# The end of the gap between two scans: 1 + e in another buffer, product buffers in the other order, the second row norm on VectorE, GpSimd's list in another order

## What is computed

```python
# mixer (per batch, channels in 8 blocks of 128, 16 states n)
delta = softplus(dt_w @ dt + dt_b)                    # (512, 1024)
h = h * exp(delta * A[n]) + (delta * u) * B[n]        # scan over 512 steps
y = sum_n h * C[n] + u * D ; y = y * silu(z) ; x = x + y @ out_w
# quantised MLP on layernorm(x), weights of this batch
x = x + smooth_quant_mlp(layernorm(x), fside, ctx)
# experts on layernorm(x): this is "the second row norm"
x = x + top2_of_16_experts(layernorm(x)) + sigmoid(gate) * shared_expert(layernorm(x))
```

## Time and profile before

| | us |
|---|---|
| median of 3 runs | 1702.78 |
| lowest, highest | 1702.05, 1710.21 |
| profiled execution | 1698.6 |
| its span, first to last instruction | 1696.8 |
| TensorE busy in it | 1445.6 |
| VectorE busy | 1349.2 |
| GpSimd busy | 1065.7 |
| ScalarE busy | 798.0 |

### The profile page before, as it was taken

One profiled execution on the slowest core, in us unless ns is written; L12 is line 12 of the kernel. 1 busy time (PEld: TensorE's weight loads), 2 busy tenths in 40 slices (PEclk: granted clock), 3 DMA queues, 4 the chain that ended last, 5 costly groups with the idle time before them and its releaser, 6 DMA issues.

```text
span 1696.8 us, 19403 instructions
## 1 busy us (share of the span) xinstructions
PE 1445.6 (85%) x5408; PEld 830.0 (49%) x5416; DVE 1349.2 (80%) x2215; ACT 798.0 (47%) x1368; POOL 1065.7 (63%) x684
## 2 busy tenths in 40 slices
PE   7867678999699899999699899999699999836994
PEld 3323223444465565444465565444465665325783
DVE  3488999676899999796899999796899999784212
ACT  3575454245734565245734565245734565222141
POOL 0299999101999899500999899500999999422101
PEclk9988899999699999999699999999699999967997
DMA  3550000412535674513535674512534774600984
GB/s 111 207 204 25 0 0 1 161 38 76 220 121 182 198 242 150 204 44 101 217 124 174 205 238 154 204 44 101 217 125 147 236 233 130 248 25 8 353 333 143
DMA packets 94074, 252.14 MB, mean 149 GB/s; under 512 B 11024, under 2 KB 11152, under 8 KB 88848
## 3 DMA queue, kind: packets, MB, share of 16 engines
q1 hardware_dynamic: 86688, 229.93, 39.9%
q0 software_dynamic: 5120, 16.78, 3.0%
q10 hardware_dynamic: 2160, 4.19, 0.6%
HBM read 207.87 MB, written 42.99 MB: 148 GB/s over the span
## 4 chain that ended last, share of the span: by engine, by line
PE 52%; DVE 18%; issue 13%; POOL 7%; ACT 7%; DMA 2%; DVEq 0%; POOLq 0%; SPq 0%; ACTq 0%
PE bank L1902 10%; PE bank L1780 6%; DVE bank L1253 6%; PE bank L2028 5%; PE bank L1795 4%; PE bank L1834 4%; PE bank L1839 4%; POOL work L659 4%; PE bank L1931 3%; PE bank L1828 3%; PE bank L1923 2%; PE bank L1803 2%; DVE work L1265 2%; PE bank L1802 2%; DVE pairs L1265 2%
## 5 line engine op out<-in xcount | busy, mean ns | idle before, releaser
L659 POOL TENSOR_TENSOR work<-du,BB 128x1024 f32<-128x1024 f32 x255 | 603.0, 2378 | 5.2 <-DVE work L1529 4.4
L926 ACT ACTIVATE bank<-delta,A_sb 128x512 f32<-128x512 f32 x512 | 349.9, 690 | 477.3 <-DVE pairs L1265 260.8
L1253 DVE TENSOR_TENSOR_SCAN bank<-bank,work 128x512 f32<-128x512 f32 x432 | 522.5, 1219 | 12.9 <-ACT bank L926 9.2
L1902 PEld LDWEIGHTS bank<-x3T,ew_up 128*128 128x128 f32 x1488 | 221.1, 196 | 74.5 <-issue 63.2
L1902 PE MATMUL bank<-x3T,ew_up 128*128 128x128 f32 (+1 forms) x1488 | 243.3, 310 | 5.2 <-issue 5.2
L1265 DVE TENSOR_TENSOR pairs<-bank,CB 128x512 f32<-128x512 f32 x240 | 160.9, 671 | 1.6 <-PE bank L1839 0.6
L604 POOL TENSOR_TENSOR col<-col,halfpow 128x4 f32<-128x4 f32 (+1 forms) x8 | 7.8, 973 | 209.8 <-DVE col L1405 209.8
L1265 DVE TENSOR_TENSOR work<-bank,CB 128x512 f32<-128x512 f32 x192 | 128.3, 668 | 0.0
L1795 PE MATMUL bank<-xT,wst 128*128 128x512 f32 x256 | 117.7, 604 | 8.4 <-ACT delta L873 6.6
L1834 PE MATMUL bank<-pairs,ident 128*128 128x512 f32 x160 | 90.6, 650 | 34.4 <-DVE zg L1273 18.8
L2028 PE MATMUL bank<-wst,zg 128*128 128x512 f32 x256 | 117.0, 593 | 0.9 <-DVE zg L1273 0.9
(11 more groups left out here) (243 smaller groups left out, 2518.2 us busy)
## 6 DMA issues: line engine op xcount, KB each, us to landing
ew_up<-in_exp_w SPq DMA_DIRECT2D x93, 512.0 KB, 3.8
ew_dn<-in_exp_w SPq DMA_DIRECT2D x93, 256.0 KB, 4.3
hm<-xs_dram SPq DMA_DIRECT2D x69, 256.0 KB, 4.6
ys_dram<-x3T SPq DMA_DIRECT2D x69, 256.0 KB, 4.5
wst<-in_w_in SPq DMA_DIRECT2D x64, 256.0 KB, 2.7
BB<-bc_dram SPq DMA_DIRECT2D x16, 1024.0 KB, 7.2
CB<-bc_dram SPq DMA_DIRECT2D x16, 1024.0 KB, 9.1
wst<-in_out_w SPq DMA_DIRECT2D x32, 256.0 KB, 2.9
```

Of the source, the lines that this page charges most:

```text
L659: nc.gpsimd.tensor_tensor(dBu[:, k % CHUNK_SLOTS, :, :], du[:, j % 2:j % 2 + 1, :].broadcast_to([P, 2, T]), BB[:, n0:n0 + 2, :], ALU.mult) ...
L926: nc.scalar.activation(R[q % RING][:, :], delta[:, j, :], ACT.Exp, scale=A_sb[:, j, n:n + 1]).then_inc(S["da_ready"], 1)
L1253: V.tensor_tensor_scan(prod[c % (2 * PAIR_SLOTS)] if on_pool(q) else R[q % RING][:, :], R[q % RING][:, :], dBu[:, c // 2 % CHUNK_SLOTS, c ...
L1902: ins = mm(gu_bank(v)[:, part * n:(part + 1) * n], w[:, part * D + k * P:part * D + (k + 1) * P], rhs, start=(k == 0), stop=(k == KD - 1))
```

## The change

1. **Buffer of 1 + e.** `sp_w` of blocks 4 to 7 is `xT`, the transposed input, in place of `late_pairs`. `one_more` of these blocks waits for all z projections, the last readers of `xT`, no longer for `softplus_less` of blocks 0 to 3.
2. **Product buffers.** `prod[0:4]` is `late_pairs`, `prod[4:8]` is `pairs`. Products 0 to 3 wait for `softplus_less` of blocks 0 to 3 and products 4 to 7 for the errors of blocks 4 to 7.
3. **VectorE** does `softplus_less` of blocks 1 to 3 (new `less`) and the second row norm (new `row_norm`: one small step for `row_shift`, four tiles of `xn`) ahead of `one_more` of blocks 4 to 7. The errors of blocks 4 to 7 move behind products 2 and 3.
4. **GpSimd** makes only the power of the second norm, and before du and chunk 0 (`row_power`). `softplus_sum` of blocks 4 to 7 follows chunk 1, and chunk 2 waits for it and for all inverses; `softplus_less` of blocks 4 to 7 is spread to steps 4, 7, 9 and 11 of the scan's pair loop.
5. **ScalarE** loses the row norm, and its four `x3` copies stand ahead of `lns` of blocks 4 to 7.

`last`, which has no scan beside it, keeps `norm` and ScalarE's `row_norm`.

```diff
+LESS_AT = {4: 4, 5: 7, 6: 9, 7: 11}
+ERROR_AT = {4: 3, 5: 3, 6: 4, 7: 4}
-        prod = [pairs[:, i, :] for i in range(4)] + [late_pairs[:, i, :] for i in range(4)]
+        prod = [late_pairs[:, i, :] for i in range(4)] + [pairs[:, i, :] for i in range(4)]
         def sp_w(a, m):
+            return late_pairs[:, m, :] if m < 4 else xT[:, m - 4, :]
# GpSimd
+            def row_power(l):
+                pool.wait_ge(S["var_ready"], l + 1)
+                nc.gpsimd.tensor_tensor(rstd[:], mv[:, :, 1], halfpow[:, 1, :], ALU.pow).then_inc(S["rstd_ready"], 2)
             def chunk(b, k):
                 if k == 2 and b > 0:
                     pool.wait_ge(S["sum_ready"], NBLK * (b + 1))
+                    pool.wait_ge(S["sp_inv_ready"], NBLK * (b + 1))
# ScalarE, between
                 for c in range(RING):
                     decay(a, c)
+                for i in range(KD):
+                    x3(a, i)
                 lns(a, range(4, 8))
-                row_norm(m, 2 * m + 1)
                 inverses(a, range(4, 8))
# VectorE
             def one_more(a, m):
                 if m >= 4:
-                    ve.wait_ge(S["delta_ready"], NBLK * a + m - 3)
+                    ve.wait_ge(S["z_ps"], NBLK * (a + 1))
+            def less(a, m):
+                ve.wait_ge(S["sum_ready"], NBLK * a + m + 1)
+                ve.wait_ge(S["sp_err_ready"], NBLK * a + m + 1)
+                ve.wait_ge(S["delta_ready"], NBLK * a + m)
+                V.tensor_tensor(delta[:, m, :], delta[:, m, :], sp_w(a, m), ALU.subtract).then_inc(S["delta_ready"], 1)
+            def row_norm(m):
+                l = 2 * m + 1
+                ve.wait_ge(S["var_ready"], l + 1)
+                ve.wait_ge(S["rstd_ready"], 2 * (l + 1))
+                V.scalar_tensor_tensor(out=row_shift[:], in0=mv[:, :, 0], scalar=-1.0, in1=rstd[:],
+                                       op0=ALU.mult, op1=ALU.mult).then_inc(S["row_shifted"], 1)
+                ve.wait_ge(S["row_shifted"], l + 1)
+                for t in range(TT):
+                    V.tensor_scalar(xn[:, t, :], x2[:, t, :], rstd[:, t:t + 1], row_shift[:, t:t + 1], ALU.mult, ALU.add
+                                    ).then_inc(S["xn_ready"], 1)
# VectorE, scan_stage: after the product of step p
-                    if scan and p == 1 and b > 0:
-                        for i in range(4, 8):
-                            softplus(b, i)
+                    for i in range(4, 8):
+                        if scan and b > 0 and p == ERROR_AT[i]:
+                            softplus(b, i)
# VectorE, between
                 row_stats(m, 2 * m + 1)
+                for i in range(1, 4):
+                    less(a, i)
+                row_norm(m)
                 for i in range(4, 8):
                     one_more(a, i)
```

## The result

| | before | changed |
|---|---|---|
| median of 6 runs each, same chip | 1705.13 us | 1726.32 us |
| lowest, highest | 1700.33, 1710.21 | 1721.44, 1729.84 |
| ratio, 95% interval | | 1.0118 [1.0098, 1.0139] |
| profiled execution, its span | 1698.6, 1696.8 | 1728.51, 1726.8 |
| granted clock | 0.931 | 0.923 |

The time went up by 21.2 us where +9.0 was forecast; 1726.3 lies outside 1695 to 1717. The sign was right, the size less than half. What follows is counted inside the three gaps, from the end of VectorE's variance step (432.70 before, 439.06 after), and leaves that out.

A forecast was written before the change was run, and what follows sets the result against it. Two chains with next to no slack bound it: VectorE through scan 5 to `posi`, GpSimd to the gates' weights. Each 3.0 us later a gap, 9.0 in three, on 1702.8 gave 1711.8 us; range 1695 to 1717.

The forecast's parts named there:

- Row norm, the port: VectorE's moved steps and GpSimd's big ones wait for each other's whole instruction; the last tile ends at 442.3.
- free port: Rival, chance 0.15: the port hardly matters for VectorE's moved steps; -3.1 us a gap, 1693.5 us.
- row norm that slips through: Rival, chance 0.24: small step and tiles hold the port ahead of chunk 1; 1700 to 1706.5 us.
- fourth rival: Chance 0.05: GpSimd's power also blocks VectorE's first `less`; 1.3 us a gap more, 1715.7 us.
- ScalarE, part 5: ScalarE waits 3.9 us for TensorE's transposes, then makes the copies first; inverses come 3.0 us later.
- Scan and errors: On VectorE each moved error meets a long GpSimd step; scan 5 starts at 464.4 instead of 461.43, +3.0 us.
- Both chains are displaced by 3.0 us a gap: The sum: VectorE at scan 5 and GpSimd at the gates' weights each 3.0 us late, 9.0 in three gaps.
- TensorE's clock: Rival, chance 0.12: matmuls ahead of the first down projection run at 1.2 GHz; 0 to 2.8 us a gap on top.
- Not on the path: Logits and the first expert's matmuls start some 6 us earlier, but next meet VectorE's routing at fixed scan steps.
- GpSimd: Chunk 2 starts 4.5 us earlier, four `softplus_less` add 5.1, waits add more; gates' weights +3.0 us.
- Only their own time: Spreading GpSimd's four `softplus_less` over later steps costs just their duration, 4 x 1.27 = 5.1 us.
- the forecast's case: VectorE and GpSimd take turns at the port, chance 0.44: 1711.8 us, own range 1709.4 to 1714.5.

The follow-up runs named there:

- experiment 10: The changed kernel with GpSimd's chunk 1 moved behind the four sums: 1730.7 us, one run.
- experiment 4: The changed kernel with GpSimd's `softplus_less` of blocks 5 to 7 at steps 18, 20, 22, behind the gates' weights: 1725.0 us, 1.0112 of the kernel before.
- 1: The changed kernel measured again, without an edit: 1728.5 us, 1.0134 of the kernel before.
- 5: The kernel before profiled again, without an edit: 1706.3 us, one run.
- 12: The kernel before, with GpSimd's chunk 14 in the first stage waiting for chunk 13 to end: 1703.7 us, 1.0002 of the kernel before.
- 8: The changed kernel with `x3` copies behind the inverses, all four errors on GpSimd behind chunk 3, and `softplus_less` later: 1706.4 us, 0.9999 of the kernel before.
- 9: As 8, but errors 4 and 5 on VectorE ahead of product 0, 6 and 7 on GpSimd: 1705.4 us, 0.9998 of the kernel before.
- 7: The changed kernel with twelve extra unused TensorE matmuls ahead of the routing's ranks: 1722.3 us, 1.0098 of the kernel before.
- 2: The changed kernel with ScalarE's `x3` copies back behind the inverses: 1716.8 us, 1.0056 of the kernel before.
- 3: As 2, with the second row norm back on ScalarE and its small steps on GpSimd: 1721.1 us, 1.0094 of the kernel before.

## Why the prediction was wrong, point by point

- **Row norm, the port: right.** Power, `less`, du and both chunks took turns as told; the last tile came 9.6 us after the variance step, where the prediction's 442.3 less 432.70 is 9.6 as well. The rivals on a free port and on the row norm that slips through are refuted by it, and experiment 10 shows the cause: 3.92 us with chunk 1, 1.91 without. The power did not block: two `less` ran beside it and the third waited for du (3.35 us for the three), so the fourth rival fell. The rule of the Trainium skill (SBUF — State Buffer, "Who interferes with whom"), that VectorE's step with two SBUF inputs contends with a GpSimd instruction that reads SBUF and the later one waits for the whole instruction, agrees with the small step's 2.29 us, but not with the `less` that ran inside the power; there the measurement decides.
- **ScalarE, part 5: mis-sized by 1.1.** The wait for the transposes and the copies are the main cause, as forecast; undoing the order gave back 11.7 us of the total. But the transposes' end 1.36 us after the last tile was taken from a trace in which ScalarE's tiles ended 0.71 us apart. VectorE's last three end 0.46 apart, and TensorE is slower than either: one transpose each 0.21 us, 16 of them in 3.34 us before and 3.56 now, counted from the first tile. So they end 2.34 after the last tile. Inverses at 21.0 instead of 19.9.
- **Scan and errors: +3.7 instead of +3.0.** From the inverses' end to scan 5 it was 11.5 us, 11.8 forecast. The errors cost 3.55 + 4.01 against 8.1. The excess is that of the inverses, less these 0.3, an error of size the other way.
- **The sum failed here: "Both chains are displaced by 3.0 us a gap".** It took the displacement at scan 5 as final. Behind it came two more terms. The first is the rival **TensorE's clock**, given 0.12 and no place in the sum, although showed the engine at 0.64 just ahead of the routing. The prediction looked at the 7.5 us of matmuls ahead of the down projections, and said against it that "between 466 and 478 there is work every few microseconds". That work was the early expert matmuls, and the change itself opened a hole behind them: with the copies early they end 3.7 us earlier, with the late scan 5 the ranks come 3.8 us later, and nothing is left between 471.8 and 479.9. The clock then strikes the ranks, between two steps of VectorE's routing, not the large matmuls: 1.43 for 0.81 us, and VectorE, which waits for them, loses 1.4 us a gap. "Not on the path" was the wrong heading for work that comes earlier.
- **GpSimd: +6.4 instead of +3.0 at the weights.** Chunk 2 was 3.2 us early (21.3 against 24.5), not 4.5, 1.1 of it again the transposes. Four `softplus_less` cost 5.5, not 5.1. The rest was put at 2.4 and came to 4.1: the first scatter waits 2.19 for the late `posi` where it was idle for 0.65 before, two pairs wait 1.25 together for products, and du, pair 0 and chunks 2 and 3 together took 1.3 more in their turns with VectorE. "Only their own time" was too much for three of the spread `softplus_less`: experiment 4 takes 3.8 us of them out and gets 1.3 back, since GpSimd's list was no longer without waits.
- **Chances.** The rivals were told as cases that exclude each other. They were not: the forecast's case and, at another place, the clock's case both came true, 9 and 4 us, the transposes added 2 and GpSimd's list 4 more, and that sum left the range.

## What to carry to other kernels

Follow a displacement to the end of the stage: at each later hand-over ask anew whether it grows, and add the rivals that can come true together before the range is drawn. Work that is moved earlier leaves a hole where it stood; look at what the engine with a variable clock does right after the hole, above all many small instructions in a chain with another engine. Where a consumer is slower than its producer, as TensorE's transposes were with both producers of the tiles, count its end from the producer's first tile: the distance from the last tile changes with the producer's pace.

## What the runs showed of the hardware that was not expected

- A two-input step of VectorE can be passed over more than once: 5.80 us behind du and two chunks without a pause (experiments 1 and 5), 3.52 with a pause of 0.17 us between the chunks (12), 1.20 when it came in behind du. Which of 1.20 and 5.80 it is varies between profiles of one program.
- It happens to GpSimd too: a sum of 1.26 us took 3.58 beside four two-input steps of VectorE that follow each other without a pause (8, and 3.49 in 9).
- Six matmuls of 48 columns took 0.81 us at 2.4 GHz and 1.43 at 1.2 GHz. After 2.88 us without work the ranks began at full clock and fell to the lower level within the first or second group of them (7), after 3.33 and 3.77 us within the first (2, 3); after 0.54 us (before) and 0.71 (3) they did not.
